# Norm weights spread by a one-row matmul and the first tile turned by TensorE, in place of a broadcast load and a transposing transfer

## The reference

```python
x = x + attention(layernorm(x), ctx, mask)

def _linear_bit(x, w, g):
    xq = _act_quant(_rmsnorm(x, g))      # g * x * rsqrt(mean(x*x) + 1e-8), then 8 bits per row
    wq = _ternary_quant(w)               # round(tanh(w / mean|w|)) * arctanh(mean|w|)
    return einsum('bsd,od->bso', xq, wq)

u = layernorm(x)
h = silu(_linear_bit(u, w1, g1)) * _linear_bit(u, w2, g2)     # the up stage, 512 -> 2048
x = x + _linear_bit(h, w3, g3)                                # the down stage, 2048 -> 512
```

## Time and profile before

| | |
|---|---|
| median of 3 runs | 444.42 us (443.5 to 445.0) |
| the profiled execution | 444.06 us |
| its span in the profile | 442.3 us |
| TensorE busy | 398.4 us, 90% |
| VectorE busy | 382.3 us, 86% |
| ScalarE busy | 343.5 us, 78% |
| GpSimd busy | 358.3 us, 81% |
| share of the 16 DMA engines, main queue | 58.5% |
| chain that ended last, by engine | PE 53%, POOL 13%, DVE 12%, ACT 10%, issue 9% |

### The profile page before, as it was taken

How to read it: one execution, slowest core, us unless ns; L and a number is a source line. 1 busy time by engine, 2 the same in 40 slices (tenths; PEclk the granted TensorE clock), 3 DMA queues, 4 the chain that set the end, 5 groups by cost and what they waited for, 6 DMA issues and landing times.

```text
span 442.3 us, 8289 instructions
## 1 busy us (share of the span) xinstructions
PE 398.4 (90%) x1870; PEld 179.0 (40%) x1870; DVE 382.3 (86%) x835; ACT 343.5 (78%) x618; POOL 358.3 (81%) x559
## 2 busy tenths in 40 slices
PE   8326596899999999999999999999999989999996
PEld 8102232334434443444344444444344443444443
DVE  5599598999799979997999979997999799798794
ACT  3677779687998789886998698878988697667661
POOL 0149888999889988898879987998889897899970
PEclk9755796999999999999999999999999999999999
DMA  6999881545675547843684568554784425354541
GB/s 256 398 333 367 282 189 24 143 90 125 171 194 103 119 105 188 184 103 81 170 194 92 117 168 189 105 119 102 183 185 103 88 66 113 80 96 101 106 103 73
DMA packets 110359, 66.40 MB, mean 150 GB/s; under 512 B 100736, under 2 KB 100864, under 8 KB 106752
## 3 DMA queue, kind: packets, MB, share of 16 engines
q1 hardware_dynamic: 110336, 66.14, 58.5%
HBM read 33.10 MB, written 8.39 MB: 94 GB/s over the span
## 4 chain that ended last, share of the span: by engine, by line
PE 53%; POOL 13%; DVE 12%; ACT 10%; issue 9%; DVEq 1%; DMA 1%; POOLq 0%; SPq 0%; ACTq 0%
PE S L1279 29%; PE DN L1312 15%; POOL stageB L549 5%; PE R L1258 3%; ACT stageB L740 3%; DVE stageB L972 3%; ACT prob L695 2%; DVE hm L978 2%; POOL c L538 2%; ACT L695 2%; PE DN L1320 1%; DVE ga L945 1%; PE R L1225 1%; ACT junk_x L718 1%; ACT sg L748 1%
## 5 line engine op out<-in xcount | busy, mean ns | idle before, releaser
L549 POOL TENSOR_TENSOR stageB<-stageB,g3b 128x512 f32<-128x512 f32 x127 | 161.9, 1289 | 7.4 <-DVE stageB L972 4.8
L1279 PE MATMUL S<-W2q,q12T 128*128 128x512 f16 x512 | 134.2, 385 | 5.3 <-DVE W2q L1044 3.3
L1279 PE MATMUL S<-W1q,q12T 128*128 128x512 f16 x512 | 135.9, 389 | 1.2 <-ACT sg L748 0.9
L1312 PE MATMUL DN<-W3q,stageB 128*128 128x512 f16 x496 | 122.2, 380 | 0.5 <-DVE W3q L1044 0.4
L748 ACT ACTIVATE sg<-S,asc 128x512 f32<-128x512 f32 x128 | 86.9, 682 | 25.5 <-PE S L1279 23.4
L972 DVE TENSOR_TENSOR stageB<-sg,S 128x512 f32<-128x512 f32 x128 | 86.1, 678 | 20.0 <-ACT sg L748 20.0
L978 DVE TENSOR_REDUCE hm<-stageB 128x1 f32<-128x512 f32 x127 | 85.9, 677 | 2.0 <-POOL stageB L549 1.9
L1279 PEld LDWEIGHTS S<-W2q,q12T 128*128 128x128 f16 x512 | 50.4, 99 | 69.4 <-DVE W2q L1044 4.5
L1279 PEld LDWEIGHTS S<-W1q,q12T 128*128 128x128 f16 x512 | 48.8, 100 | 70.2 <-issue 9.2
L1312 PEld LDWEIGHTS DN<-W3q,stageB 128*128 128x128 f16 x496 | 47.9, 98 | 59.1 <-issue 1.1
L755 ACT ACTIVATE junk<-stageB 128x1024 bf16<-128x1024 f32 x64 | 67.3, 1051 | 4.3 <-DVE stageB L972 4.2
(11 more groups left out here) (127 smaller groups left out, 431.1 us busy)
## 6 DMA issues: line engine op xcount, KB each, us to landing
X<-in_x SPq DMA_DIRECT2D x8, 1024.0 KB, 6.3
out_x<-X SPq DMA_DIRECT2D x32, 256.0 KB, 2.7
xTs<-in_xT SPq DMA_DIRECT2D x7, 1024.0 KB, 7.2
X<-in_w1T SPq DMA_DIRECT2D x4, 1024.0 KB, 10.7
stageB<-in_w2T SPq DMA_DIRECT2D x4, 1024.0 KB, 18.5
X<-in_w3T SPq DMA_DIRECT2D x4, 1024.0 KB, 9.2
ctxr<-in_ctx SPq DMA_DIRECT2D x16, 128.0 KB, 3.0
ctxc<-in_ctx SPq DMA_DIRECT2D x8, 128.0 KB, 4.4
```

The lines of the kernel that those rows point to most:

```text
L549: nc.gpsimd.tensor_tensor(gh[q][:, part], hp[:, part], g3b[:, part], ALU.mult).then_inc(s_gh_made, 1)
L1279: mm = nc.tensor.matmul(bank[n % 2][:, :], q12T[q][:, i * KD + k, :], w[:, n, k, :], start=(k == 0), stop=(k == KD - 1))
L1312: mm = nc.tensor.matmul(bank[:, :], src[:, k, :], W3q[:, k, :], start=(k == 0), stop=(k == KH - 1))
```

## The change

It does these things:

1. Ten of the 20 matmuls ahead of the program's work are taken out.
2. `g1` and `g2` are loaded as one row each, into partition 0 of `sg[0]` and `sg[1]`, and SP issues the two loads right after `load_x(0)`, ahead of all weights. TensorE multiplies each row by a row of ones into R[0] and R[1] (128x512, one row of the array in use), and ScalarE copies the two results to `g12b`. VectorE's `stage_a_gain(0)` waits for these copies.
3. `transpose_12(0, 0)` is taken out of SP's program. TensorE turns the first `c12` with eight float16 transposes into bank S2[0] (`turn_12`), and ScalarE copies the bank to `q12T[0]` (`turned_12`). The other 31 tiles still take the transposing DMA. What counted its completions counts one fewer, and `quantize_12(1)` waits for TensorE's transposes.

```diff
             load_ctxc(0)
             load_x(0)
+            for i, g in enumerate((g1, g2)):
+                sp.dma_start(sg[i][0:1, :], g.partition_broadcast(1)).then_inc(s_gains_in, 16)
             for k in range(WC):
                 load_w(stageA, w1T, k, w_in[0][k])
                 if k == 1:
                     load_ctxr(0)
-                if k == 2:
-                    for i, g in enumerate((g1, g2)):
-                        sp.dma_start(g12b[:, i, :], g.partition_broadcast(P)).then_inc(s_gains_in, 16)
...
             load_ctxc(1)
-            transpose_12(0, 0)
             sp.dma_start(g3b[:, :], g3.partition_broadcast(P)).then_inc(s_gain3_in, 16)
...
             def quantize_12(t):
                 pool.wait_ge(s_a_f, 2 * (t + 1))
-                if later(t):
-                    pool.wait_ge(s_q12_in, 16 * t)
+                if later(t, 2):
+                    pool.wait_ge(s_q12_in, 16 * (t - 1))
+                elif t == 1:
+                    pool.wait_ge(s_turn_12, 1)
...
+            def turned_12():
+                act.wait_ge(s_turn_12, 1)
+                nc.scalar.copy(q12T[0][:, :, :].rearrange("p k q -> p (k q)"), q12P).then_inc(s_q12_turned, 1)
...
             table(0, ACT.Exp)
+            for i in range(2):
+                act.wait_ge(s_gains_ps, i + 1)
+                nc.scalar.copy(g12b[:, i, :], R[i][:, :]).then_inc(s_gains_made, 1)
             attention_ccT(0)
...
             weight_abs(1, stageB[:, :], 2, s_w2_abs)
+            turned_12()
             weight_abs(1, stageB[:, :], 3, s_w2_abs, WN // 2)
...
-            dve.wait_ge(s_gains_in, 32)
+            dve.wait_ge(s_gains_made, 2)
             stage_a_gain(0)
...
+            def turn_12():
+                pe.wait_ge(s_ident_h, 1)
+                pe.wait_ge(s_c12_made, 2)
+                for k in range(HB):
+                    mm = nc.tensor.transpose(q12P[:, k * P:(k + 1) * P], c12[:, k * P:(k + 1) * P], ident16[:, :])
+                mm.then_inc(s_turn_12, 1)
...
-            for i in range(20):
+            for i in range(10):
                 nc.tensor.matmul(DN[:, 0:P], ones[:, :], ones[:, :], start=True, stop=True)
+            pe.wait_ge(s_gains_in, 32)
+            for i in range(2):
+                nc.tensor.matmul(R[i][:, :], ones[0:1, :], sg[i][0:1, :], start=True, stop=True).then_inc(s_gains_ps, 1)
             attention_ccT(0)
...
             attention_readout(0, 1)
+            turn_12()
             weight_total(1, s_w2_abs, WC + 1)
```

More of the change, by code:

```diff
@@ L172, in bit_ffn_xattn @@
         xP = S1 + S2
+        q12P = S2[0][:, :].bitcast(F16)
         q3P = [bank[:, :].bitcast(F16) for bank in (S1[0], S1[1], S2[0])]
@@ L187, in bit_ffn_xattn @@
         s_gains_in = sem("gains_in")
+        s_gains_ps = sem("gains_ps")
+        s_gains_made = sem("gains_made")
         s_ctxc_in = sem("ctxc_in")
@@ L261, in bit_ffn_xattn @@
         s_q12_in = sem("q12_in")
+        s_turn_12 = sem("turn_12")
+        s_q12_turned = sem("q12_turned")
         s_up1_ps = sem("up1_ps")
@@ L1267, in weight_total @@
                 nc.tensor.matmul(DN[:, 0:parts], ones[:, :], wabs[:, i, 0:parts], start=True, stop=True).then_inc(s_w_tot, 1)
+            def turn_12():
[4 more added lines that the diff above has]
+                mm.then_inc(s_turn_12, 1)
             def up(t, n, q):
-                if n == 0:
-                    pe.wait_ge(s_q12_in, 16 * (t + 1))
+                if n == 0 and later(t):
+                    pe.wait_ge(s_q12_in, 16 * t)
+                elif n == 0:
+                    pe.wait_ge(s_q12_turned, 1)
                 for i, (bank, w, wq, done, used) in enumerate(((S1, W1q, s_w1_q, s_up1_ps, s_silu_made),
```

## The result

The changed kernel is slower. The median of its runs was 448.62 us (447.16 to 450.18) against 444.42 us, a ratio of 1.0100 with a 95% interval of 1.0073 to 1.0127. Of the 30 runs of the kernel before beside e1 to e4, one took 839.53 us and stands in no ratio.

What follows compares the result with a forecast made beforehand. The prediction took the start-up chain of waits, from TensorE's first work to GpSimd's first quantized tile, as the bound. +1.85 us on 444.06 gives 445.9; with the median 0.36 above that execution, it forecast 446.3 us, range 444.2 to 449.2.

Steps and rivals of the forecast that it cites:

- the first term: TensorE's start-up: gain matmuls run before the context, so turn_x starts at 10.35 us instead of 8.50, +1.85 us.
- rival 1: TensorE's clock falls in the idle gap after the shortened warm-up: slower by some 4 us, 448.4 us; chance 0.33.
- the forecast: Whole kernel: only the +1.85 us start-up delay counts, giving 446.3 us; chance 0.42.
- The rows land with `x`: Start-up loads: the gain rows, issued behind x, land at 8.05 us, bounds 6 and 8.7.
- The two matmuls: TensorE's start-up: the two one-row gain matmuls run in sequence and take 1.9 us, all on the path.
- ScalarE's copies, the transposing transfer, SP's queue: ScalarE's gain copies, the first tile's transposing DMA replaced, and SP's earlier issues: each costed at 0.
- The bound of +0.5 for ScalarE's new place: ScalarE at 31 to 34 us, held for the q12T copy: cost 0, at most +0.5 us.
- Rival 1's price: Start-up at 1.2 GHz until just after the gains: 1.85 + 1.7 + 0.3 = 3.9 us, taken as 4.
- an upper figure of 7 us: Start-up: the delay if the clock comes back only after the scores, because transposes don't count as busy.
- Rival 2: Clock holds until the readout, saving 1.2 us on probabilities and readout: +0.65 us, 445.1 us, not measurable; chance 0.18.
- Rival 3: Gain rows land before about 6.1 us, matmuls leave the path, clock holds to the readout: -1.2 us, 443.2 us; chance 0.07.
- TensorE finishes its warm-up at 8.0 us, exactly when x lands: Start-up of the kernel before: no slack ahead of x, so the gain matmuls' time comes on top.

Runs made afterwards that it cites:

- e1: The changed kernel with all 20 warm-up matmuls back, nothing else: 446.48 us against 444.25 for the kernel before, ratio 1.0049.
- e4: The changed kernel with 20 warm-up matmuls, one-row gain matmuls moved behind attention_turn(0), ScalarE's copies behind its attention_probT(0): 444.25 us, ratio 0.9997.
- e8: The changed kernel, 10 warm-up matmuls, with the gain matmuls over all 128 rows instead of one: 446.62 us, ratio 1.0043.
- e9: The changed kernel timed once more, unaltered: 449.15 us against 444.30 for the kernel before, ratio 1.0109.
- e3: The kernel before with only the first tile turned by TensorE and ScalarE, 20 warm-up matmuls, broadcast gain loads: 443.82 us, ratio 0.9991.
- e7: e4 with the gain matmuls over all 128 rows instead of one, sg zeroed first: 443.24 us against 444.55 for the kernel before, ratio 0.9972.
- e6: The changed kernel, 10 warm-up matmuls, with the two gain rows issued ahead of all other loads: 446.56 us, ratio 1.0035.
- e2: The kernel before with 10 warm-up matmuls instead of 20, nothing else: 445.14 us, ratio 1.0026.
- e5: The kernel before with ten unread full-array matmuls between attention_turn(0) and attention_probT(0): 443.73 us against 444.55, ratio 0.9981.
- e11: e7 with 15 warm-up matmuls instead of 20: 442.62 us, ratio 0.9963 against the kernel before.
- e10: The kernel before with 15 warm-up matmuls instead of 20: 443.44 us against 444.30, ratio 0.9983.

## Why the prediction was right, and where it was not

The direction, the place and the first term were right; the time came out where rival 1 had put it (448.4), not at the forecast (446.3), and inside the range, whose upper end was drawn for that rival. The forecast's +1.85 us is less than half of the +4.2 measured, and the second measurement, 449.15, lies 0.05 us below the range's end. That rival 1's price fits is in part luck, as shown below.

- *The rows land with `x`.* Forecast 8.05 us; TensorE's first gain matmul started at 8.05. TensorE began on the rows 0.02 us before VectorE began on `x` in the change's profile and 0.12 before it in e8, but 0.33 us behind it in e9. The Trainium skill, "DMA: Bandwidth & Descriptors", section "Queues, rings and completion order", says that completion is not first in, first out; these profiles show the rows next to `x`, on either side of it.
- *The two matmuls.* Forecast 1.9 us, in sequence; 1.98 us. `turn_x` started at 10.49 on the chain against a forecast 10.35, so the +1.85 us were +1.99.
- *ScalarE's copies, the transposing transfer, SP's queue:* all 0, as costed: none of them stands in the chain up to `c`. e3 measures the third part at -0.4 us, with 0 at the edge of its interval. The bound of +0.5 for ScalarE's new place was not reached: the logarithm lost its whole 1.44 us of idle time, and no more.
- *The clock.* The step that failed is the choice between the forecast and rival 1: "The price of that is the clock, which is the first rival", at 0.33. In both profiles of the change the clock fell behind the gap and `turn_x` took 3.4 and 3.2 us instead of 1.90, +1.5 and +1.3. The prediction had the warm-up end at 5.5 us, 2.5 us ahead of the rows, and took the idle time to be over with the gain matmuls. Its own have the slow records some 0.23 us apart, not 0.21, and the ten matmuls, all at 1.2 GHz, ended at 6.2 us; TensorE was idle for 1.89 us. The clock rose at 6.8, during that idle time, and the gain matmuls ran at full speed behind it, but they did not keep it up. That one-row matmuls do not keep the clock as the same matmuls over all rows do is shown by e4 against e7, in the traces and in the times, and by e6, where the clock fell behind 3.08 busy microseconds. The idle stretch has its part: e1, with one-row matmuls and no idle time, kept the clock to 17.3 us, and so did e2, to 17.0, with idle time and no one-row matmuls. How the loss divides between the two in the change stays open; e8 is faster in its runs, but its one profile doesn't show by what.
- *Rival 1's price* was 4 us; +4.2 and +4.9 us were measured. But it was made of other terms. The prediction took 1.7 us more for gain matmuls at 1.2 GHz and 0.3 for the context, with full speed from there on; in the profile the gain matmuls ran at 2.4 GHz, and the transposes, which the 4 us left at full speed, took 1.5 us more. Of the profiled 3.3 us, 2.0 are the gain matmuls, 1.5 the transposes, less 0.25 for the turning of the probabilities. The two medians lie 0.9 and 1.6 us above this. I take it for executions in which the clock did not rise in the warm-up at all, where the gain matmuls too would run at 1.2 GHz; neither of the two profiles caught one, so that is argued and not shown. That the price and the median agree is therefore luck as far as the profile goes.
- *A rule that did not hold.* The Trainium skill, "TensorE: Matmul & The Clock Gate", section "Part 4: PE-mode transpose", says that transposes don't count as busy in the same way, from which I drew an upper figure of 7 us. In the changed profile the clock rose at 13.6 us, and from 10.0 to that moment TensorE had done nothing but transposes, all float32. The measurement decides.
- *Rival 2* needed the clock to hold from the dense work to the readout. In the change it held for the probabilities (0.45 us) and fell just before the readout (2.10 us for the pair), and it holds for both when the gap behind `attention_turn(0)` is filled with full-array matmuls: e5, e7 and e11, 1.13 us.
- *Rival 3* needed the rows by 6.1 us. e6 put them there, and found -1.2 us wrong: +1.6 us by the ratio, +2.0 by the medians, because with ten warm-up matmuls and one-row matmuls the clock falls anyway.
- *"TensorE finishes its warm-up at 8.0 us, exactly when x lands"* was true of the one profile I had. In those of e1, e3, e4, e5 and e7 it ended at 8.6 to 8.9 us. The kernel before carried a loss of its own there. e10, without the overrun, is 0.8 us faster (0.1 to 1.4 by its interval), but its profile shows that gain at the readout and not ahead of `turn_x`, so the size of the overrun's part stays open.

## What to carry to other kernels

Work put ahead of the first useful matmul is on the path as far as it runs past the landing of that matmul's data: all of the two gain matmuls in the change and in e1, none of them in e6. A warm-up should be judged by when it ends at either clock, not by what one profile shows: with 20 matmuls it overran the data in five of six profiles, by 0.4 to 0.9 us, and with ten the change lost the clock. A small matmul that spreads a row is free in a gap that TensorE spends waiting for another engine, and there it can be made to do a second job.

The fastest version has loads of one row, the spreading matmul in the gap and over all rows of the array, the first tile turned by TensorE, and a warm-up of 15; it is 1.7 us under the kernel before. Most or all of that may not come from the change's own parts. The one-row loads and the turned tile together brought nothing that can be measured (e4, ratio 0.9997). e5 (matmuls that nothing reads, in the gap) and e10 (a warm-up of 15) have none of the change's parts and brought 0.8 us each. The kernel before with both was not run, so this simpler rival stays untested.

## What the runs showed of the hardware that I had not expected

- Two matmuls of 512 columns with one row in use (1.98 us) were followed by a fall of the clock near 17.0 us in e4; the same two over all 128 rows, 127 of them zeros (1.88 us), by none until 20.5 us in e7. Against the kernel before, the times differ by 1.1 us (ratios 0.9997 and 0.9972, intervals apart).
- The clock can fall while TensorE is busy. In e6 it rose at 5.71 us and fell at 9.12, and between the two TensorE was busy for 3.08 us, 1.98 of them with one-row matmuls. In e2 it rose at 6.75 us, TensorE was busy for 2.41 us up to 10.10, without such matmuls, and the clock fell only at 17.0.
- The moment at which the clock first rises differs from one execution to the next, with a warm-up that always starts at 1.53 us: 5.4 us in the profile of before, 5.7 to 7.5 us in the others. Alone it moves the end of 20 warm-up matmuls from 8.1 to 8.9 us.
